# A vision tower on one core: the expert row buffer zeroed in another order, and unread products on TensorE behind the convolution

## The chip, the cores and the metric

The program runs on one of the eight cores of a Trainium2 chip, in one launch. The time is device microseconds of an execution, and a kernel's time is the median of its runs. Three runs of the kernel before took 235.38, 237.4 and 239.8 us, median 237.4.

## The reference

128 images of 64x64x3 go through a small vision tower. Each image gives 16 tokens of 128 features, 2048 tokens in all, everything in float32.

```python
y = conv(concat(x, four shifts of x), 16x16 patches) + conv_b     # 2048 x 128
h = layernorm(y) * gamma + beta;  h = h @ dense_w + dense_b
n = layernorm(h)                                                  # retention with 8 heads
h = h + silu(n @ wg.T + bg) * (decayed (q k') v)
n = layernorm(h)                                                  # 64 experts, top 2
buf[expert, position] = n   for both chosen experts (at most 256 rows each)
y = (silu(buf @ w1) * (buf @ w3)) @ w2                            # for each expert
h = h + weighted sum of the token's two expert rows + shared expert(n)
```

Rows of `buf` that no token fills are zero in the reference.

## The kernel before, in words

The program is written engine by engine, in an order set by hand; semaphores connect the engines. Nothing is scheduled by a planner.

**Attention phase.** The tokens form 16 tiles of 128. A loop of 21 steps (`for i in range(LAST)`) is written out on TensorE (PE), ScalarE (ACT), VectorE (DVE) and GpSimd (POOL). In step i, TensorE works on several tiles at different depths: `attend(i - 3)`, `embed(i + 1)` (lines 429 and 430), `places(i - 5)`, `scores(i - 2)` (line 473), `turn(i)` (two transposes, lines 441 and 444), `logits(i - 4)` (line 507) and `project(i - 1)` (lines 451 to 460). The convolution (line 419) is cut in four groups of four tiles, each of eight matmuls of 512 columns; `conv_step` puts two of them in each step, one at the step's start and one behind `turn`, so that group 1 is done in steps 0 to 2, group 2 in steps 3 to 6 and group 3 in steps 7 to 10. From step 11 on `conv_step` does nothing. A float32 matmul is two instructions in the trace.

GpSimd does in step i `rstd(i)` (lines 1054 to 1058: the inverse deviations of three layer norms, for which the vector engine and the scalar engine of the step wait), and then two `send(i - 6, k)` (line 1069): indirect DMAs that scatter a tile's 128 normalized rows to their places in the row buffer `buf` in DRAM (`expert_rows` in the trace), one for each of the two chosen experts. It works in order, so that a send that waits holds up the next `rstd`.

**The row buffer.** `buf` has 64 experts x 256 rows of 512 bytes (8 MiB), an overflow part and a drop part. It is zeroed from a tile of zeros, `fill` (128 partitions x 16 rows; the trace calls it EW, since it lies in that tensor), by DMAs that SyncE (SP) issues at line 328: eight, each on 128 partitions, where partition p writes rows 16n to 16n+15 of its own 128 rows. The first send waits for all eight (`pool.wait_ge(filled, 16 * FILLS)`). Before the fills SP waits for all four parts of the images of group 1 (`X` in three parts on 128 partitions, line 307, and `XE`, the edge pixels, on 96 partitions, line 309); the images of group 2 are issued behind the first fill, those of group 3 behind the last. SP's queue is worked off in order.

**Turnover.** Behind step 20 TensorE counts the rows of each expert (line 567). SP waits for all sends and then loads the rows of the first experts (line 352); the first transposes of the **expert phase** (line 575) wait for them. That phase takes 17 blocks of 4 experts through line 575 (transpose), 583 and 596, then comes the shared expert (lines 517 to 523), while GpSimd gathers the result rows (line 1097) and the output is stored.

Of the kernel before, what the change touches and what calls it, by code (L numbers as in the profile page):

```python
# [30 lines left out]
P = 128  # L31
# [68 lines left out]
def tower(nc, xp, xe, wp, we, sq, w13, w2, vecs, rows, cst, out):  # L100
    ctx = ExitStack()
    with ctx:
# [3 lines left out]
        def sem(name):  # L106
            return ctx.enter_context(nc.semaphore(name))
# [115 lines left out]
        wp_in = [sem(f"wp_in{n}") for n in range(NL)]  # L223
        x_in = [[sem(f"x_in{n}_{part}") for part in range(NL + 1)] for n in range(2)]
        filled_tile, filled = sem("filled_tile"), sem("filled")
        spare_filled, drop_filled = sem("spare_filled"), sem("drop_filled")
        ones_set = sem("ones_set")
        w_ready, wd_in_ready, wd_ps, wd_ready, cvec_ready, bqm_ready, before_ready = (sem(n) for n in (
            "w_ready", "wd_in_ready", "wd_ps", "wd_ready", "cvec_ready", "bqm_ready", "before_ready"))
# [55 lines left out]
        def turns(i):  # L285

            return min(max(i - FIRST2 + 1, 0), LAST2 - FIRST2 + 1)
        FILLS = NE * CAP // P // FILLR
        SPARES = NOV * BLK // P // FILLR
        PACE = 6  # L290
        assert FILLS * FILLR * P == NE * CAP and SPARES * FILLR * P == NOV * BLK

        def first_blocks(g):

# [4 lines left out]
        def _(sp):  # L299
# [16 lines left out]
            sp.dma_start(R[:, :], rows.partition_broadcast(P)).then_inc(r_in, 16)  # L316
            load_group(1)
            sp.dma_start(decay, cst[:, NC_CONST - NC_DECAY:]).then_inc(decay_in, 16)
            for part in range(NL + 1):
                sp.wait_ge(x_in[1][part], 16)  # L320
            sp.wait_ge(filled_tile, 1)
            sp.dma_start(buf[SLOTS:ROWS], fill[:, 0]).then_inc(drop_filled, 16)
            main = buf[0:NE * CAP].rearrange("(p r) w -> p r w", p=P)
            spare = buf[NE * CAP:SLOTS].rearrange("(p r) w -> p r w", p=P)
            for n in range(FILLS):
                if n == 1:
                    load_group(2)
                sp.dma_start(main[:, n * FILLR:(n + 1) * FILLR], fill[:, :, :]).then_inc(filled, 16)
            load_group(3)
            for n in range(SPARES):  # L330
                sp.wait_ge(y_ps, PACE + n)
# [2 lines left out]
            def load_weights():  # L334

                for n in range(NWL):
                    c = slice(n * WEX, (n + 1) * WEX)
                    sp.wait_ge(y_ps, PACE + SPARES + n)
                    sp.dma_start(EW[:, 0, c], w13[c].rearrange("e d n -> d e n")).then_inc(w13_in[n], 16)
                sp.wait_ge(w_ready, NL)  # L340
                sp.wait_ge(filled, 16 * FILLS)
                sp.wait_ge(spare_filled, 16 * SPARES)
                for n in range(NWL):
                    c = slice(n * WEX // PE_EX, (n + 1) * WEX // PE_EX)
                    sp.wait_ge(y_ps, PACE + SPARES + NWL + n)
                    sp.dma_start(EW[:, 1, c], w2.rearrange("(q a) h n -> (a h) q n", a=PE_EX)[:, c]
                                 ).then_inc(w2_in[n], 16)
# [56 lines left out]
        def _(pe):  # L404
            def conv(g, j):

                if j % HC == 0:
                    pe.wait_ge(x_in[g % 2][j // HC], 16 * (g // 2 + 1))
                    if g == 0 and j < NCH:
                        pe.wait_ge(w_ready, j // HC + 1)  # L410
                    if g == 0 and j == NCH:
                        pe.wait_ge(we_in, 16)
                if j == 0 and g >= 1:
                    pe.wait_ge(yT_ready, g)
                if j < NCH:
                    w, x = W[:, j], X[:, g % 2, j]
                else:
                    w, x = WE[:, j - NCH], XE[:, g % 2, j - NCH]
                mm = nc.tensor.matmul(CONV[:, :], w, x, start=(j == 0), stop=(j == NCH + 1))  # L419
                if j == NCH + 1:  # L420
                    mm.then_inc(conv_ps, 1)
# [112 lines left out]
            pe.wait_ge(wd_ready, 1)  # L534
            pe.wait_ge(cvec_ready, 1)

            def conv_step(i, n):

                g, j = (i + 1) // TG + 1, 2 * ((i + 1) % TG) + n
                if i == 0:  # L540
                    conv(g, n)
                if g < NG:
                    conv(g, j)

            embed(0)
            for i in range(LAST):
                conv_step(i, 0)
                if 0 <= i - 3 < NT:
                    attend(i - 3)
                if i + 1 < NT:  # L550
                    embed(i + 1)
                if 0 <= i - 5 < NT:
                    places(i - 5)
                if 0 <= i - 2 < NT:
                    scores(i - 2)
                if FIRST2 <= i <= LAST2:
                    turn(i)
                conv_step(i, 1)
                if 0 <= i - 4 < NT:
                    logits(i - 4)  # L560
                if 0 <= i - 1 < NT:
                    project(i - 1)
# [3 lines left out]
            for k in range(TOPK):  # L566
                mm = nc.tensor.matmul(O[:, 0:NE], ones[:, :], acc[:, NT % 3, k], start=(k == 0), stop=(k == TOPK - 1))
            mm.then_inc(count_ps, 1)

            def turn_rows(q, u, v=0, first=False, back=2):  # L570

# [447 lines left out]
        @block.gpsimd  # L1019
        def _(pool):  # L1020
            steps = [0]

            def own(ins):

                steps[0] += 1
                ins.then_inc(pool_step, 1)
                pool.wait_ge(pool_step, steps[0])

            pool.memset(fill[:, :, :], 0.0).then_inc(filled_tile, 1)
            pool.memset(mhalf[:, :], -0.5)  # L1030
            pool.memset(MV[:, :, :, :], 1.0)
            pool.memset(EPS[:, 0:1], LN_TOK)
            pool.memset(EPS[:, 1:3], LN)
            pool.memset(bvg[:, :], 0.0)
            own(pool.memset(ones[:, :], 1.0))
            pool.sem_inc(ones_set, 1)
            pool.wait_ge(c_in, 16)
            pool.memset(acc[:, 0, 1], 0.0)
            pool.tensor_scalar(acc[:, 0, 0], expert, CAP / P, None, ALU.mult).then_inc(base_ready, 1)

            def rstd(i):

                if i < NT:
                    pool.wait_ge(ystat, i + 1)
                if 0 <= i - 1 < NT:
                    pool.wait_ge(hstat, i)
                if 0 <= i - 4 < NT:
                    pool.wait_ge(h2stat, i - 3)
                if 0 <= i - 3 < NT:
                    pool.wait_ge(xn_ready, i - 2)  # L1050
                if 0 <= i - 6 < NT:
                    pool.wait_ge(xf_ready, i - 5)
                b = i % 2
                own(pool.tensor_tensor(VE[:, :], MV[:, b, :, 1], EPS[:, :], ALU.add))  # L1054
                own(pool.tensor_tensor(RS[:, b], VE[:, :], mhalf[:, :], ALU.pow))  # L1055
                pool.sem_inc(rs_ready, 1)
                for k in (1, 2):
                    ins = pool.tensor_scalar(NM[:, b, k:k + 1], MV[:, b, k, 0:1], RS[:, b, k:k + 1], -1.0,  # L1058
                                             ALU.mult, ALU.mult)
                ins.then_inc(nm_ready, 1)  # L1060

            def send(t, k):

                pool.wait_ge(slot_ready, t + 1)
                pool.wait_ge(xf_ready, t + 1)
                if t == 0:
                    pool.wait_ge(filled, 16 * FILLS)
                    pool.wait_ge(drop_filled, 16)
                pool.indirect_dma_start(  # L1069
                    buf, bass.IndirectOffsetOnAxis(ap=slots[:, k, t:t + 1], axis=0),  # L1070
                    xrow[:, t % XR], None).then_inc(sent[t % XR], 16)

            for i in range(LAST):
                if i <= LAST2:
                    rstd(i)
                if 0 <= i - 6 < NT:
                    for k in range(TOPK):
                        send(i - 6, k)
            for k in range(TOPK):
                send(NT - 1, k)  # L1080


            for q in range(OVER):
                pool.wait_ge(ys_ready, q + 1)
                pool.dma_start(first_blocks(group(q)), ys[:, q % NY]).then_inc(put[q % NY], 16)  # L1085
            more = pool.value_load(ovn[0:1, 0:1], min_val=0, max_val=NOV // EG - 1)
            for n in range(MORE):
                with pool.If(more > n):
                    pool.wait_ge(put_over, 16 * EG * (n + 2))
            pool.wait_ge(put_over, 16 * EG)  # L1090
            pool.wait_ge(put_late, 16 * (NB - 1 - OVER))
            for z in range(NY):
                pool.wait_ge(put[z], 16 * stores(NY * NB + z))
            pool.wait_ge(conv_ps, NG)
            for t in range(NT):
                for k in range(TOPK):
                    pool.indirect_dma_start(  # L1097
                        pr[:, t, k], None, buf,
                        bass.IndirectOffsetOnAxis(ap=slots[:, k, t:t + 1], axis=0)).then_inc(pr_in[t // TS], 16)
# [53 lines left out]
```

## Time and profile before

| | |
|---|---|
| runs | 235.38, 237.4, 239.8 us; median 237.4 |
| profiled execution | 236.28 us, its span 234.5 us |
| mean granted TensorE clock | 0.842 |
| TensorE matmul, busy | 163.5 us (70%) |
| VectorE, busy | 135.6 us (58%) |
| GpSimd, busy | 107.2 us (46%) |
| DMA | 42.96 MB, mean 183 GB/s |

The span runs from the first to the last instruction; 1.8 us of the execution's time lie around it. The page cuts the span into 40 slices of 5.86 us. The attention phase takes the slices up to about 136 us, the expert phase those from 143 to 182, and the gather the rest. The granted clock has two levels: 1.00 is 2.4 GHz and 0.50 is 1.2 GHz.

### The profile page before, as it was taken

What the parts mean: (1) busy time and instruction counts of PE and PEld (TensorE: products, weight loads), DVE (VectorE), ACT (ScalarE), POOL (GpSimd) and SP (SyncE); (2) the same over time, 40 slices, a digit from 0 to 9 for tenths busy, and PEclk for the clock granted to TensorE, in tenths of its full rate; (3) what the DMA queues carried; (4) which work ended last, traced back from release to release, by engine and by line L of the source; (5) the groups of instructions that cost most, each with busy time, mean ns of one, the idle gap of its engine ahead of it and who ended that gap; (6) DMA issues with size and microseconds to landing.
All of it is one profiled execution on the core that took longest, in us unless ns stands there. A gap on an engine that the chain in (4) does not pass through costs nothing.

```text
span 234.5 us, 4462 instructions
## 1 busy us (share of the span) xinstructions
PE 163.5 (70%) x1402; PEld 113.3 (48%) x1402; DVE 135.6 (58%) x487; ACT 83.7 (36%) x229; POOL 107.2 (46%) x169
## 2 busy tenths in 40 slices
PE   0888899997999987888988305999998655530000
PEld 0334455664666655656575204888887433320000
DVE  1525646684768898886447781577777422229222
ACT  2010565555256676653552202555554101100000
POOL 4004322225836666675446750133330077777760
PEclk9999999999599999975555555999999999995555
DMA  6999799999998744300000118699742612224421
GB/s 245 390 315 291 231 379 422 425 414 361 389 289 227 225 141 130 117 22 25 22 22 15 35 45 246 170 257 286 249 121 81 192 41 55 56 52 121 118 73 34
DMA packets 29213, 42.96 MB, mean 183 GB/s; under 512 B 2752, under 2 KB 21376, under 8 KB 27904
## 3 DMA queue, kind: packets, MB, share of 16 engines
q1 hardware_dynamic: 26176, 35.27, 45.0%
q0 software_dynamic: 3008, 7.34, 10.6%
q8 instruction: 13, 0.21, 0.4%
q14 instruction: 16, 0.13, 0.2%
HBM read 24.45 MB, written 18.15 MB: 182 GB/s over the span
## 4 chain that ended last, share of the span: by engine, by line
PE 32%; DMA 21%; POOL 14%; issue 10%; DVE 8%; SPq 8%; ACT 3%; POOLq 1%; DVEq 0%; ACTq 0%
POOL X L1097 12%; DMA expert_rows<-EW 10%; DMA XE<-xe 6%; PE bank L583 5%; PE scores L484 5%; PE bank L575 4%; PE scores L473 3%; PE conv_counts L419 3%; DVE go L837 2%; SPq L307 2%; DMA expert_rows<-ys 2%; PE bank L459 2%; PE bank L507 2%; POOL expert_rows L1069 2%; PE scores L596 2%
## 5 line engine op out<-in xcount | busy, mean ns | idle before, releaser
L1097 POOL DMA_INDIRECT X<-expert_rows,slots x32 | 30.6, 956 | 21.8 <-DMA expert_rows<-ys 12.3
L1069 POOL DMA_INDIRECT expert_rows<-xrow,slots x32 | 32.4, 1013 | 14.6 <-issue 8.3
L419 PE MATMUL conv_counts<-X,W 128*128 128x512 f32 x48 | 26.9, 666 | 8.0 <-DVE W L776 6.6
L688 ACT ACTIVATE qm<-bank,bqm,C 128x128 f32<-128x128 f32 x64 | 24.1, 460 | 7.0 <-PE bank L452 7.0
L484 PEld LDWEIGHTS scores<-vg,ST 64*64 64x64 f32 x512 | 19.4, 156 | 10.2 <-issue 10.2
L973 DVE TENSOR_TENSOR hT<-bank,gs 64x256 f32<-64x256 f32 x34 | 14.5, 427 | 15.1 <-ACT gs L745 14.7
L1085 POOL DMA_DIRECT2D expert_rows<-ys x12 | 9.1, 762 | 27.5 <-DVE ys L987 27.5
L484 PE MATMUL scores<-vg,ST 64*64 64x16 f32 x512 | 20.9, 222 | 0.7 <-DVE ST L884 0.2
L1054 POOL TENSOR_TENSOR VE<-MV,EPS 128x3 f32<-128x3 f32 x20 | 4.0, 199 | 36.6 <-issue 15.2
L1055 POOL TENSOR_TENSOR RS<-VE,mhalf 128x3 f32<-128x3 f32 x20 | 17.8, 889 | 1.6
L837 DVE TENSOR_TENSOR go<-scores,vg 64x128 f32<-64x128 f32 x32 | 9.1, 286 | 15.3 <-PE scores L484 15.1
L583 PE MATMUL bank<-xbT,EW 128*128 128x128 f32 x128 | 17.9, 285 | 0.0
L737 ACT ACTIVATE xbT<-bank 128x512 f32<-128x512 f32 x17 | 10.2, 597 | 20.5 <-PE bank L575 20.5
L575 PE MATMUL bank<-C,xb 128*128 128x128 f32 x68 | 11.7, 302 | 7.4 <-DMA xb<-expert_rows 7.4
L661 ACT ACTIVATE xT<-bank 128x256 f32<-128x256 f32 (+1 forms) x19 | 6.7, 351 | 28.0 <-PE bank L444 22.6
L583 PEld LDWEIGHTS bank<-xbT,EW 128*128 128x128 f32 x128 | 16.4, 200 | 0.4 <-issue 0.3
L1010 DVE SCALAR_TENSOR_TENSOR h<-X,pw,h 128x128 f32<-128x128 f32 x32 | 9.5, 349 | 11.7 <-DMA X<-expert_rows,slots 9.6
L419 PEld LDWEIGHTS conv_counts<-X,W 128*128 128x128 f32 x48 | 8.6, 212 | 15.1 <-DMA X<-xp 11.4
L473 PE MATMUL scores<-qm,kT 64*64 64x256 f32 x128 | 12.5, 462 | 4.6 <-DVE go L837 4.5
L745 ACT ACTIVATE gs<-bank 64x512 f32<-64x512 f32 x17 | 10.0, 589 | 6.7 <-PE bank L583 6.6
L575 PEld LDWEIGHTS bank<-C,xb 128*128 128x128 f32 x68 | 7.8, 150 | 9.4 <-DMA xb<-expert_rows 7.6
L1058 POOL TENSOR_SCALAR NM<-MV,RS 128x1 f32<-128x1 f32 x40 | 10.3, 271 | 4.2 <-POOL RS L1055 4.2
(129 smaller groups left out, 338.1 us busy)
## 6 DMA issues: line engine op xcount, KB each, us to landing
expert_rows<-EW SPq DMA_DIRECT2D x10, 1024.0 KB, 17.8
X<-xp SPq DMA_DIRECT2D x12, 512.0 KB, 10.8
xb<-expert_rows SPq DMA_DIRECT2D x16, 256.0 KB, 4.1
expert_rows<-ys POOLq DMA_DIRECT2D x12, 256.0 KB, 3.3
EW<-w SPq DMA_DIRECT2D x4, 512.0 KB, 4.3
EW<-wp SPq DMA_DIRECT2D x3, 640.0 KB, 6.4
XE<-xe SPq DMA_DIRECT2D x4, 384.0 KB, 13.0
expert_rows<-ys SPq DMA_DIRECT2D x4, 256.0 KB, 3.0
```

What stands on the lines that cost most here:

```text
L419: mm = nc.tensor.matmul(CONV[:, :], w, x, start=(j == 0), stop=(j == NCH + 1))
L473: mm = nc.tensor.matmul(S[toks, n, 0:QM * TB], kT[rows, t % 2, toks], qm[rows, t % 2, :, toks], start=True, stop=True)
L484: mm = nc.tensor.matmul(S[toks, c, AVC + hh * HD:AVC + (hh + 1) * HD], ST[toks, t % 2, hh], vg[toks, t % 4, hh * HD:(hh + 1) * HD], start= ...
L575: mm = nc.tensor.transpose(XT[u][:, e * BLK:(e + 1) * BLK], xb[:, v, e], ident)
L583: mm = nc.tensor.matmul(GU[u][:, e * BLK:(e + 1) * BLK], w[:, e], xbT[:, u, e], start=True, stop=True)
L688: nc.scalar.activation(qm[:, t % 2, m], QK[:, 0:P], ACT.Identity, bias=bqm[:, m:m + 1], scale=head[:, m:m + 1])
L837: ins = nc.vector.tensor_tensor(go[toks], S[toks, c, AVC:AVC + P], vg[toks, t % 4, P:2 * P], ALU.mult)
L973: ins = nc.vector.tensor_tensor(hT[a * HID:(a + 1) * HID, u], up[:, a], gate[:, a], ALU.mult)
L1055: own(pool.tensor_tensor(RS[:, b], VE[:, :], mhalf[:, :], ALU.pow))
L1058: ins = pool.tensor_scalar(NM[:, b, k:k + 1], MV[:, b, k, 0:1], RS[:, b, k:k + 1], -1.0, ALU.mult, ALU.mult)
L1069: pool.indirect_dma_start(buf, bass.IndirectOffsetOnAxis(ap=slots[:, k, t:t + 1], axis=0), xrow[:, t % XR], None).then_inc(sent[t % XR], 16)
L1097: pool.indirect_dma_start(pr[:, t, k], None, buf, bass.IndirectOffsetOnAxis(ap=slots[:, k, t:t + 1], axis=0)).then_inc(pr_in[t // TS], 16)
```

## The change

There are two edits, and a few lines that serve them.

1. **The fills.** The same 8 MiB are now zeroed by 16 DMAs of 64 partitions. Each writes 16 rows of every one of the 64 experts; fill n takes its zeros from partitions 0 to 63 where n is even and 64 to 127 where it is odd. The first eight cover rows 0 to 127 of each expert and count on `filled`, the other eight count on a new semaphore `filled_rest`. The first send (tile 0) waits for the first eight alone, the sends of tile 1 for the rest; the load of the second projection's weights waits for both. SP begins the fills when two of the four parts of group 1's images have landed, no longer all four. The images of group 2 are issued behind two of the new fills, which is as many bytes as before; those of group 3 still behind the last.
2. **The products.** `idle_product` multiplies a convolution weight with 256 columns of weights (float32) into the PSUM bank of the convolution, and nothing reads the result. From step 11 on it stands in both places of `conv_step`; from step 16 on there is a third behind `places`; and 12 follow behind the count of rows. In all there are 37. The first waits for the last convolution result to be read out.

```diff
+        filled_rest, spare_filled, drop_filled = sem("filled_rest"), sem("spare_filled"), sem("drop_filled")
...
-        FILLS = NE * CAP // P // FILLR
+        FILLS = CAP // FILLR
+        FIRST_FILLS = P // FILLR
...
+        TURNOVER = 12
...
-            for part in range(NL + 1):
+            for part in range(NL - 1):
                 sp.wait_ge(x_in[1][part], 16)
...
-            main = buf[0:NE * CAP].rearrange("(p r) w -> p r w", p=P)
+            main = buf[0:NE * CAP].rearrange("(e r) w -> e r w", e=NE)
             for n in range(FILLS):
-                if n == 1:
+                if n == 2:
                     load_group(2)
-                sp.dma_start(main[:, n * FILLR:(n + 1) * FILLR], fill[:, :, :]).then_inc(filled, 16)
+                half = slice(n % 2 * NE, (n % 2 + 1) * NE)
+                sp.dma_start(main[:, n * FILLR:(n + 1) * FILLR], fill[half]
+                             ).then_inc(filled if n < FIRST_FILLS else filled_rest, 16)
             load_group(3)
...
+            def idle_product(i, n):
+                if i == NT - TG - 1 and n == 0:
+                    pe.wait_ge(yT_ready, NG)
+                nc.tensor.matmul(CONV[:, 0:2 * P], W[:, 0], W[:, 1:3], start=True, stop=True)
+
             def conv_step(i, n):
                 g, j = (i + 1) // TG + 1, 2 * ((i + 1) % TG) + n
+                if g >= NG:
+                    return idle_product(i, n)
...
                 if 0 <= i - 5 < NT:
                     places(i - 5)
+                if i >= NT:
+                    idle_product(i, 2)
...
             mm.then_inc(count_ps, 1)
+            for n in range(TURNOVER):
+                idle_product(LAST, n)
...
                 if t == 0:
-                    pool.wait_ge(filled, 16 * FILLS)
+                    pool.wait_ge(filled, 16 * FIRST_FILLS)
                     pool.wait_ge(drop_filled, 16)
+                if t == 1:
+                    pool.wait_ge(filled_rest, 16 * (FILLS - FIRST_FILLS))
```

The first place is SyncE's queue in the attention phase, from the wait for group 1's images to the load of group 3 (line 307 or 309 is X, 309 or 311 is XE, 328 or 331 the fills). Before:

```order
L322 DMA expert_rows<-EW 128x128 [waits x_in1_3,x_in1_2,filled_tile,x_in1_1,x_in1_0]
L328 DMA expert_rows<-EW 128x2048
L307 DMA X<-xp 128x1024 [waits conv_ps]
L307 DMA X<-xp 128x1024 x2
L309 DMA XE<-xe 96x1024
L328 DMA expert_rows<-EW 128x2048 x7
L307 DMA X<-xp 128x1024 [waits conv_ps]
```

Now:

```order
L324 DMA expert_rows<-EW 128x128 [waits filled_tile,x_in1_1,x_in1_0]
L331 DMA expert_rows<-EW 64x2048 x2
L309 DMA X<-xp 128x1024 [waits conv_ps]
L309 DMA X<-xp 128x1024 x2
L311 DMA XE<-xe 96x1024
L331 DMA expert_rows<-EW 64x2048 x14
L309 DMA X<-xp 128x1024 [waits conv_ps]
```

The order of the queue is the same; the fills are twice as many at half the partitions, and the queue starts on two parts of group 1.

The second place is TensorE in the second half of step 16 and the start of step 17. Before:

```order
L473 MATMUL scores<-qm,kT 64x256 x3
L441 MATMUL bank<-C,xrow 128x128 [waits xf_ready,th_ready,xT_ready]
L444 MATMUL bank<-C,xn 128x128 [waits xn_ready]
L507 MATMUL bank<-SQ,xT 128x64 [waits xT_ready]
L451 MATMUL bank<-xT,SQ 128x128 [waits qk_ready,xT_ready]
L452 MATMUL bank<-xT,SQ 128x128
L459 MATMUL bank<-SQ,xT 128x256 [waits g_ready,vg_ready]
L460 MATMUL bank<-bvg,ones 128x256
L484 MATMUL scores<-vg,ST 64x16 [waits st_ready,vg_ready]
```

Now:

```order
L546 MATMUL conv_counts<-W 128x256
L478 MATMUL scores<-qm,kT 64x256 [waits av_read,st_ready,qk_ready]
L478 MATMUL scores<-qm,kT 64x256 x3
L446 MATMUL bank<-C,xrow 128x128 [waits xf_ready,th_ready,xT_ready]
L449 MATMUL bank<-C,xn 128x128 [waits xn_ready]
L546 MATMUL conv_counts<-W 128x256
L512 MATMUL bank<-SQ,xT 128x64 [waits xT_ready]
L456 MATMUL bank<-xT,SQ 128x128 [waits qk_ready,xT_ready]
L457 MATMUL bank<-xT,SQ 128x128
L464 MATMUL bank<-SQ,xT 128x256 [waits g_ready,vg_ready]
L465 MATMUL bank<-bvg,ones 128x256
L546 MATMUL conv_counts<-W 128x256
```

Three products (L546) have come into a step: ahead of the scores, between the transposes and the logits, and ahead of the next step's attention matmuls (L484, L489 in the changed kernel).

## Rows read from the trace of the kernel before

**Rows 1.** Page, 40 slices of the span: TensorE's granted clock in tenths.

```profile
PEclk9999999999599999975555555999999999995555
```

**Rows 2.** Timeline at the first send: start, us, engine, line, operation, idle before.

```profile
48.08 0.16 DVE L863 SCALAR_TENSOR_TENSOR slots<-over,pos 128x2 uint32<-128x2 f32 x1
...
54.61 1.23 POOL L1069 DMA_INDIRECT expert_rows<-xrow,slots  x1 [5.42 <-DVE slots L863]
...
58.88 0.45 PE L429 MATMUL bank<-C,yT 128*128 128x128 f32 x1 [1.82 <-DVE h L871]
```

**Rows 3.** Timeline of PE: embedding matmuls of four steps, tiles 7 to 10.

```profile
51.01 0.39 PE L430 MATMUL bank<-WD,yT 128*128 128x128 f32 x2
...
59.12 0.63 PE L430 MATMUL bank<-WD,yT 128*128 128x128 f32 x2
...
67.40 0.39 PE L430 MATMUL bank<-WD,yT 128*128 128x128 f32 x2
...
73.19 0.39 PE L430 MATMUL bank<-WD,yT 128*128 128x128 f32 x2
```

**Rows 4.** Chain that ended last: start, us, what.

```profile
30.91 22.66 DMA expert_rows<-EW
```

**Rows 5.** Page, DMA issues: out<-in, queue, count, KB each, us to landing.

```profile
expert_rows<-EW SPq DMA_DIRECT2D x10, 1024.0 KB, 17.8
X<-xp SPq DMA_DIRECT2D x12, 512.0 KB, 10.8
...
XE<-xe SPq DMA_DIRECT2D x4, 384.0 KB, 13.0
```

**Rows 6.** Windows: us, busy time of each engine, clock, DMA share, GB/s.

```profile
45.00:50.00 5.00, 4.82 (x42) 2.92 (x40) 4.40 (x20) 2.68 (x9) 1.56 (x4) 1.00 1.01 421
20.50:22.50 2.00, 2.00 (x8) 1.02 (x7) 1.65 (x7) 0.00 (x0) 0.72 (x4) 1.00 1.01 209
32.00:33.50 1.50, 1.50 (x27) 0.74 (x27) 0.00 (x0) 1.50 (x7) 0.00 (x0) 1.00 0.92 276
55.50:57.00 1.50, 1.50 (x34) 1.01 (x32) 0.00 (x0) 1.09 (x5) 1.20 (x2) 1.00 1.09 243
```

**Rows 7.** Timeline of PE's weight loads: convolution matmuls that waited for image data.

```profile
20.11 0.30 PEld L419 LDWEIGHTS conv_counts<-X,W 128*128 128x128 f32 x2 [1.00 <-DMA X<-xp]
...
54.89 0.30 PEld L419 LDWEIGHTS conv_counts<-X,W 128*128 128x128 f32 x2 [0.47 <-DMA X<-xp]
```

**Rows 8.** Timeline: scores matmuls, last statistics, last send, first expert transpose.

```profile
95.67 0.66 PE L473 MATMUL scores<-qm,kT 64*64 64x256 f32 x8 [0.39 <-DVE go L837]
...
101.00 0.66 PE L473 MATMUL scores<-qm,kT 64*64 64x256 f32 x8 [0.39 <-DVE go L837]
...
122.92 1.13 PE L473 MATMUL scores<-qm,kT 64*64 64x256 f32 x8 [0.46 <-DVE go L837]
...
129.03 0.18 DVE L849 BATCH_NORM_AGGREGATE MV<-stats 128x2 f32<-128x6 f32 x1
...
137.93 0.96 POOL L1069 DMA_INDIRECT expert_rows<-xrow,slots  x1 [0.30 <-issue]
...
143.22 1.97 PE L575 MATMUL bank<-C,xb 128*128 128x128 f32 x8 [7.40 <-DMA xb<-expert_rows]
```

**Rows 9.** Windows: three in which the granted clock changed, and a full-clock stretch.

```profile
58.00:58.50 0.50, 0.00 (x0) 0.00 (x0) 0.12 (x1) 0.00 (x0) 0.30 (x1) 0.61 1.15 451
102.50:103.00 0.50, 0.50 (x3) 0.50 (x3) 0.43 (x2) 0.00 (x0) 0.42 (x2) 0.50 0.00 0
146.50:147.00 0.50, 0.50 (x5) 0.50 (x4) 0.00 (x0) 0.00 (x0) 0.00 (x0) 0.64 1.06 280
95.00:100.00 5.00, 3.93 (x58) 2.76 (x56) 4.51 (x21) 3.13 (x11) 3.32 (x6) 1.00 0.45 136
```

**Rows 10.** Timeline of PE: a 256-column f32 product and the matmul behind it.

```profile
76.27 0.60 PE L459 MATMUL bank<-SQ,xT 128*128 128x256 f32 x2
76.70 0.27 PE L460 MATMUL bank<-bvg,ones 96*128 96x256 bf16 x1
```

More of the change, by code:

```diff
@@ L225, in tower @@
         filled_tile, filled = sem("filled_tile"), sem("filled")
-        spare_filled, drop_filled = sem("spare_filled"), sem("drop_filled")
+        filled_rest, spare_filled, drop_filled = sem("filled_rest"), sem("spare_filled"), sem("drop_filled")
         ones_set = sem("ones_set")
@@ L287, in turns @@
             return min(max(i - FIRST2 + 1, 0), LAST2 - FIRST2 + 1)
-        FILLS = NE * CAP // P // FILLR
+        FILLS = CAP // FILLR
+        FIRST_FILLS = P // FILLR
         SPARES = NOV * BLK // P // FILLR
         PACE = 6
-        assert FILLS * FILLR * P == NE * CAP and SPARES * FILLR * P == NOV * BLK
+        TURNOVER = 12
+        assert FILLS * FILLR == CAP and SPARES * FILLR * P == NOV * BLK
         def first_blocks(g):
@@ L340, in load_weights @@
                 sp.wait_ge(w_ready, NL)
-                sp.wait_ge(filled, 16 * FILLS)
+                sp.wait_ge(filled, 16 * FIRST_FILLS)
+                sp.wait_ge(filled_rest, 16 * (FILLS - FIRST_FILLS))
                 sp.wait_ge(spare_filled, 16 * SPARES)
@@ L535, in _ @@
             pe.wait_ge(cvec_ready, 1)
+            def idle_product(i, n):
+                if i == NT - TG - 1 and n == 0:
+                    pe.wait_ge(yT_ready, NG)
+                nc.tensor.matmul(CONV[:, 0:2 * P], W[:, 0], W[:, 1:3], start=True, stop=True)
             def conv_step(i, n):
                 g, j = (i + 1) // TG + 1, 2 * ((i + 1) % TG) + n
+                if g >= NG:
+                    return idle_product(i, n)
                 if i == 0:
                     conv(g, n)
-                if g < NG:
-                    conv(g, j)
+                conv(g, j)
             embed(0)
```

## The prediction

> **What bounds the kernel now.** I read the page's slices first: TensorE's granted clock stands at full speed except in one slice near 60 us, in the seven from about 103 to 146 us, and at the end [rows 1]. The timeline of the embedding matmuls then gives the length of a step: tiles 9 and 10 are 5.79 us apart, which is a step with two convolution matmuls on a full TensorE; but tiles 7 to 9 took 16.39 us instead of 11.58, so 4.8 us were lost between 51 and 67 us [rows 3]. The timeline around the first send says why: its slots were written by 48.24 us, but it started at 54.61, because the chain of waits has the last fill issued at 30.91 and landed at 53.57 [rows 2, 4]. Behind that send stands the next `rstd`; TensorE sat idle 1.82 us for what it gives, and between 58.0 and 58.5 the clock went from 2.4 to 1.2 GHz [rows 2, 9]. From step 11 on, at full clock, a step takes 5.33 us: scores at 95.67 and 101.00 [rows 8]. There VectorE, busy 4.51 of 5 us, sets the pace, and TensorE waits for it (0.39 us ahead of the scores) [rows 8, 9]. At 102.5 the clock halved with no long pause before it [rows 9], and TensorE became the bound: three steps took 21.92 us, 101.00 to 122.92 [rows 8]. The expert phase begins at 143.22, when the last sends have landed and the rows are loaded, at half clock until about 146.6 [rows 8, 9].
>
> **Fills, the wait that goes.** If group 3's images and the fills come in time, the 4.8 us are all gained: the sends themselves (2.6 us a step on GpSimd) also stand in the steps of 5.79.
>
> **Fills, the wait that may come.** All hangs on the rate of a DMA on 64 partitions, which the trace doesn't have. Two bounds: DMAs on 128 partitions move 421 GB/s, and the loads of XE, on 96, were each time a dip with the DMA engines as busy as ever: 209, 276 and 243 GB/s, mean 243 [rows 6]. The packets of X and XE have the same length, so what differs is the partitions. A 64-partition fill should alone be no better than the lowest, 209. But fills alternate between halves, and an engine that has run ahead finds the other half free, so some of the way to 421 may be regained. I take **250**, nearest to the XE rows, and keep 209 and 421 as ends.
>
> SP may start at about 20.1 us, when TensorE's wait for the second part of group 1 ended [rows 7]; but the DMA engines are busy with XE until 22.5 [rows 6] and then with 0.3 MB of decay constants and drop rows, so I count from 23.4. A fill is 64 x 16 x 512 bytes = 0.524 MB; a part of X the same; XE 0.39 MB [rows 5]. At 250 GB/s for fills and XE and 410 for X: two fills 4.2 us (27.6), X of group 2 3.8 (31.4), XE 1.6 (33.0), six fills 12.6 (45.6), eight fills 16.8 (62.4), the first part of group 3 1.3 (**63.7**). The first send, asked for at about 49.3, waits no more. The sends of tile 1, asked for at about 55, wait to 62.4, and what is queued behind them is `rstd(8)`; but the images are later still. TensorE wants group 3 at 54.4 (it stood 0.47 us for it and started at 54.89 [rows 7]), and would now stand until 63.7, **9.3 us**. Everything of the step is behind this matmul, since TensorE works in order. After a pause of this kind the clock is at half; before, the pause cost 2.3 us up to tile 8, and the slow stretch behind it another 2.5 [rows 3], which I charge again. Tile 9 then comes at 62.6 + 9.3 + 2.5 = 74.4 instead of 67.40: **+7.0 us**. At 421 for fills and 243 for XE the first part of group 3 lands at about 50.4, before it is wanted: **-4.8**. At 209 it lands at 70.4: tile 9 at 81.1, **+13.7**.
>
> The Trainium skill (SBUF — State Buffer, "Door 1: The DMA port swizzle") says that partitions 0 to 63 reach only 8 of SBUF's 16 ports, gives 196 GB/s for 64 partitions against 328 for 128 at 1 MiB with an asymptote of 218, and says that two DMAs on the two halves still serialize. It speaks against this change; the dips at XE agree with it, no row of before has a 64-partition DMA. By 218 the first part of group 3 would come at 68.8 and the time would be an estimated 241.3.
>
> **The products while the clock is full.** One costs 0.43 us of TensorE (a 256-column float32 matmul to the next) [rows 10]. The one behind `turn` lies beside ScalarE's copy of the transposes, for which TensorE idles about as long. The one ahead of the attention matmuls delays them 0.2 to 0.3 us, which VectorE's pace hides in steps 12 to 14. The first waits for the last read-out of the convolution: up to 0.5 us once, I charge **0.3**.
>
> **The products and the clock.** The clock fell at 102.5 with TensorE busy 79% of the stretch before it, and did not fall in the convolution steps, where it was busy 96% [rows 9, 6]. The products bring 0.86 us of work into a step of 5.33, where two convolution matmuls had brought 1.7. I take it that the clock holds through steps 11 to 20. Then steps 15 to 17 take no more than 5.33 us each, 16.0 instead of 21.92: **-5.9**. From the scores of tile 15 (122.92) to its last statistics (129.21) there are 6.3 us, with one set of attention matmuls at 1.9 us for 1.1: **-0.8**. From the statistics to the last send (137.93) GpSimd is the chain (an `rstd` and six sends), and from there to 143.22 two DMAs: no change. The 12 products last 5.2 us behind the count, which in the timeline began 7.7 us before the rows landed, so that a pause of 2.5 us is left, and in the pause of 1.82 us the clock went to half [rows 2, 9]; of the 1.7 us that 3.4 us at half clock can cost, I take **-0.7**, ends 0 and -1.7. What is late next is the expert rows themselves, which no product moves. Together **-7.1**.
>
> The expert phase behind it, the shared expert and the gather run as before.
>
> **Sum.** 236.28 (the profiled execution, 1.1 below the median) + 7.0 - 7.1 = **236 us**: both edits work as written, and the images of group 3, queued behind the fills, give back what the clock brings.
>
> **Rivals.**
> 1. **The halves run at full rate.** For it: fills follow each other without a gap, so that both halves can be in flight; the order of the queue is kept; every row of the 128-partition fills shows 410 to 421. Against it: the XE dips. Time 236.28 - 4.8 - 7.1 = **224.4**.
> 2. **Slower: the halves stay in step.** All engines are on the same half at any time, the rate is 209, and TensorE stands at group 3's first matmul until 70.4. Time 236.28 + 13.7 - 7.1 = **242.9**. Below about 250 GB/s the change is slower than before, above it faster; for it: the lowest dip, 2.0 us at 209 GB/s, is the bytes of one whole XE. The port rule cited above is this rival.
> 3. **The clock doesn't hold.** Products are paid at half clock (0.86 us each, one a step on the path, three steps) and the 7.1 don't come: 236.28 + 7.0 + 2.6 = **245.9**, or 234 with full-rate fills. Against it: TensorE nearly always busy at half clock got its clock back each time (146.6).
>
> **How the numbers follow.** Forecast (fills at 220 to 320 GB/s) 0.40, rival 1 0.38, rival 2 0.15, rival 3 0.07. A change of 2% is about what this measurement can tell: faster means below 232.7, slower above 242.1. Of the forecast's 0.40, 0.08 lies below 232.7 (fills at 280 or more, group 3 some 4 us earlier), 0.30 within, 0.02 above. Rival 1 is faster. Of rival 2, 0.11 is slower and 0.04 within; of rival 3, 0.05 slower and 0.02 within. So faster 0.46, same 0.36, slower 0.18. The range 223 to 242 leaves out 0.05 below and some 0.15 above; the forecast's own range is 231 to 240.
>
> **What would show it.** In the profile of the changed kernel: the DMA rate between 34 and 60 us (250 here; 410 and the matmul of group 3 without a wait for rival 1; 209 and a wait to 70 for rival 2); a long wait of TensorE for X at about 54 us; the first send without a wait for fills; a granted clock of 1.00 from step 11 to the count, and scores 5.3 us apart in steps 15 to 17; the first expert transpose 6.7 us sooner after the last embedding. I would be wrong by a term not listed if group 2's images came late (wanted at about 31.7, here 28.9), or if the products pushed the attention matmuls past VectorE's slack, which would show as steps over 5.33.

## The result, and the profile after

The changed kernel took 223.85 us (median of 4 runs, 222.81 to 225.16), the kernel before 236.59 beside it (4 runs, 235.38 to 239.8): ratio 0.948, 95% interval 0.940 to 0.956. The forecast was 236; what came was rival 1, 224.4. On another chip, where the kernel before takes 262.7 us, the same change gave only 0.986 (0.981 to 0.992); a section below is about that.

The page of the changed kernel: TensorE's granted clock in 40 slices, and SP's two kinds of fill and the images (KB each, us from issue to landing).

```profile
PEclk9999999999999999999999996999999999996555
...
expert_rows<-EW SPq DMA_DIRECT2D x16, 512.0 KB, 9.6
X<-xp SPq DMA_DIRECT2D x12, 512.0 KB, 10.6
```

The seven slices at half clock of [rows 1] are gone but for one. Now the question on which the forecast hung, the rate of DMAs on 64 partitions. Windows of the changed kernel, columns as in [rows 6]; the first is half fills, half other transfers, the other two are fills alone:

```profile
22.00:24.00 2.00, 2.00 (x6) 0.76 (x4) 1.83 (x7) 0.00 (x0) 1.20 (x2) 1.00 1.09 318
40.00:45.00 5.00, 4.70 (x47) 2.78 (x45) 3.64 (x15) 2.68 (x10) 1.64 (x4) 1.00 1.00 418
45.00:50.00 5.00, 4.82 (x48) 3.08 (x44) 4.08 (x19) 2.68 (x10) 1.56 (x4) 1.00 1.00 413
```

From 34 to 50 us the fills moved 414 GB/s, where the kernel before had 421 in its window of 45 to 50 us [rows 6]. GpSimd at the first send (start, us, engine, line, operation, idle before), and TensorE's first matmul of group 3:

```profile
49.05 0.50 POOL L1074 TENSOR_SCALAR NM<-MV,RS 128x1 f32<-128x1 f32 x2 [0.21 <-POOL RS L1071]
50.07 1.23 POOL L1087 DMA_INDIRECT expert_rows<-xrow,slots  x1 [0.52 <-issue]
```

```profile
55.87 1.12 PE L424 MATMUL conv_counts<-X,W 128*128 128x512 f32 x2 [0.70 <-DMA X<-xp]
```

The send waits for no fill (5.42 us in [rows 2]); TensorE waits 0.70 us for the images of group 3 where 9.3 were forecast. The embedding matmuls of tiles 7 to 10, to be held against [rows 3]:

```profile
51.38 0.39 PE L435 MATMUL bank<-WD,yT 128*128 128x128 f32 x2
58.13 0.39 PE L435 MATMUL bank<-WD,yT 128*128 128x128 f32 x2
63.92 0.39 PE L435 MATMUL bank<-WD,yT 128*128 128x128 f32 x2
69.71 0.39 PE L435 MATMUL bank<-WD,yT 128*128 128x128 f32 x2
```

Tile 9 comes at 63.92 for 67.40, 3.5 us sooner. Of the 4.8 lost before, 0.96 stayed in the step from 51.38 to 58.13 (6.75 for 5.79), where TensorE waits for group 3, and this run was 0.4 behind at tile 7. Now the late steps, the same places as [rows 8]: scores matmuls, last statistics, last send, first expert transpose.

```profile
97.66 0.66 PE L478 MATMUL scores<-qm,kT 64*64 64x256 f32 x8 [0.28 <-DVE go L853]
...
113.47 0.66 PE L478 MATMUL scores<-qm,kT 64*64 64x256 f32 x8
...
118.80 0.18 DVE L865 BATCH_NORM_AGGREGATE MV<-stats 128x2 f32<-128x6 f32 x1
...
127.95 0.96 POOL L1087 DMA_INDIRECT expert_rows<-xrow,slots  x1 [0.30 <-issue]
...
133.21 0.66 PE L591 MATMUL bank<-C,xb 128*128 128x128 f32 x4 [2.31 <-DMA xb<-expert_rows]
```

Three steps take 15.81 us for 21.92, the tail to the last statistics 5.33 for 6.11. The windows of the changed kernel that answer to [rows 9]:

```profile
95.00:100.00 5.00, 4.68 (x62) 3.40 (x61) 4.47 (x22) 3.27 (x11) 3.36 (x6) 1.00 0.21 68
133.50:134.00 0.50, 0.36 (x4) 0.13 (x2) 0.00 (x0) 0.10 (x1) 0.00 (x0) 0.98 0.94 249
134.00:137.00 3.00, 2.94 (x14) 2.94 (x15) 0.00 (x0) 1.18 (x3) 0.00 (x0) 0.50 1.00 280
```

With the products TensorE is busy 4.68 of 5 us for 3.93, and the clock is 1.00 through all steps. It falls once, at 134.0, after the wait of 2.31 us for the first expert's rows. The gather begins 11.0 us earlier, after a slightly shorter expert phase:

```profile
176.91 1.03 POOL L1115 DMA_INDIRECT X<-expert_rows,slots  x1 [11.55 <-DMA expert_rows<-ys]
```

The same line of the kernel before:

```profile
187.90 1.03 POOL L1097 DMA_INDIRECT X<-expert_rows,slots  x1 [12.35 <-DMA expert_rows<-ys]
```

From the first expert transpose to here it is 43.70 us for 44.68. All of it adds up: 3.5 (stall of the first send) + 6.1 (steps 15 to 17) + 0.8 (tail) + 1.0 (expert phase), less 0.4 (0.14 in the steps from tile 9 to the scores at 97.66, where the first product's wait lies, and 9.15 us from statistics to last send for 8.90) = 11.0, and the profiled executions are 11.1 apart (236.28 and 225.16). This sum is read from one pair of traces; the two edits were not run apart on a chip with these times.

The 1.0 us of the expert phase is not the clock's. The last down product (the third kind of matmul in a block) in the kernel before and in the changed one:

```profile
182.04 0.71 PE L596 MATMUL scores<-EW,hT 64*128 64x128 f32 x8 [1.02 <-DVE hT L973]
```

```profile
171.85 0.71 PE L612 MATMUL scores<-EW,hT 64*128 64x128 f32 x8 [1.02 <-DVE hT L989]
```

It comes 38.82 us behind the first expert transpose before and 38.64 now, so TensorE's blocks gained 0.2 us. The other 0.8 lies between it and the gather, where GpSimd waits 11.55 us for the last result rows to be stored, 12.35 before. The kernel with no products at the turnover (below) has 11.56 there too, so the 12 products are not its cause; what is, stays open.

### The profile page after: what moved, and what is told of

Read it like the earlier page. It is cut to its first block, busy times and chain, and to the rows that moved or that the text cites. A ratio compares the mean times of both kernels' runs of the same rounds, so it can differ in the third digit from the quotient of the medians.

```text
span 223.4 us, 4617 instructions
## 1 busy us (share of the span) xinstructions
PE 166.6 (75%) x1476; PEld 115.5 (52%) x1476; DVE 135.3 (61%) x487; ACT 83.7 (37%) x229; POOL 107.2 (48%) x169
## 4 chain that ended last, share of the span: by engine, by line
PE 35%; POOL 16%; DMA 15%; SPq 14%; issue 10%; DVE 4%; ACT 3%; POOLq 1%; DVEq 0%; ACTq 0%
POOL X L1115 13%; DMA X<-xp 11%; SPq L331 8%; PE bank L599 7%; PE bank L591 5%; PE scores L489 3%; PE conv_counts L424 3%; PE scores L478 3%; SPq L309 3%; PE scores L612 3%; DVE go L853 2%; PE conv_counts L546 2%; PE conv_counts L612 2%; POOL expert_rows L1087 2%; ACT qm L704 2%
## 5 line engine op out<-in xcount | busy, mean ns | idle before, releaser
L489 PEld LDWEIGHTS scores<-vg,ST 64*64 64x64 f32 x512 | 16.2, 134 | 9.4 <-issue 8.6
L546 PE MATMUL conv_counts<-W 128*128 128x256 f32 x74 | 20.7, 390 | 0.0
L489 PE MATMUL scores<-vg,ST 64*64 64x16 f32 x512 | 17.7, 207 | 0.6 <-DVE ST L900 0.6
L1026 DVE SCALAR_TENSOR_TENSOR h<-X,pw,h 128x128 f32<-128x128 f32 x32 | 9.5, 350 | 10.8 <-DMA X<-expert_rows,slots 8.6
L853 DVE TENSOR_TENSOR go<-scores,vg 64x128 f32<-64x128 f32 x32 | 9.2, 286 | 10.3 <-PE scores L489 10.0
L478 PE MATMUL scores<-qm,kT 64*64 64x256 f32 x128 | 10.6, 398 | 3.6 <-DVE go L853 3.4
L546 PEld LDWEIGHTS conv_counts<-W 128*128 128x128 f32 x74 | 12.2, 192 | 1.6 <-ACT yT L660 0.2
```

What stands on the lines that cost most here:

```text
L478: mm = nc.tensor.matmul(S[toks, n, 0:QM * TB], kT[rows, t % 2, toks], qm[rows, t % 2, :, toks], start=True, stop=True)
L489: mm = nc.tensor.matmul(S[toks, c, AVC + hh * HD:AVC + (hh + 1) * HD], ST[toks, t % 2, hh], vg[toks, t % 4, hh * HD:(hh + 1) * HD], start= ...
L546: nc.tensor.matmul(CONV[:, 0:2 * P], W[:, 0], W[:, 1:3], start=True, stop=True)
```

## The experiments

### The rate of the halves, and the parts one by one

These four ran on one chip, on which the kernel before took 262.65 us (19 runs, 259.88 to 264.81). Their expectations were worked out for a kernel before of 236.6 us, so that only differences and ratios can be held against them.

**All fills from partitions 0 to 63.** This leaves sizes, count and order of the DMAs as they are and takes away the alternation.

```diff
-                half = slice(n % 2 * NE, (n % 2 + 1) * NE)
+                half = slice(0, NE)
```

> All 16 fills take their zeros from partitions 0 to 63; everything else is the changed kernel. Theory (a fill on 64 partitions alone runs at half rate, and only the alternation of the halves brings the rate back to 410): between 34 us and the end of the fills the DMAs move about 210 GB/s, the 16 fills need some 40 us instead of 29, TensorE stands at the first matmul of group 3 until about 69 to 71 us, and the time is about 241 to 243 us. Rival (64 partitions are as fast as 128, and the dips at XE have another cause): 410 GB/s as in the changed kernel, no wait over 1 us for group 3, time 224 us.

Measured: 273.17 us (270.67 to 274.58), ratio 1.043 (1.026 to 1.061). Windows of this kernel, at the fills and at the stall behind them:

```profile
50.00:55.00 5.00, 3.18 (x50) 1.93 (x48) 2.57 (x11) 1.92 (x7) 2.19 (x2) 0.87 1.00 208
60.00:65.00 5.00, 0.00 (x0) 0.00 (x0) 0.00 (x0) 1.52 (x6) 0.00 (x0) 0.50 0.99 217
```

and its longest wait of TensorE (us in total, times, longest):

```profile
PE conv_counts L424 <- DMA X<-xp: 10.5, 1, 10.5
```

Fills on one half move 206 to 217 GB/s from 40 to 65 us; with the halves in turn, 408 to 426 (35 to 45 us) on this chip and the next as well. Fills on one half have half the rate, and with the halves in turn they have all of it. The stall of rival 2 is real and looks much as that rival described it: TensorE waits 10.5 us for group 3, until 70.24 us (rival 2 had 70.4), with the clock at half. It comes when all fills are on one half. The kernel is 10.5 us slower than the one before on this chip (273.17 for 262.65); the expectation had 4 to 6, and the whole change was not run on this chip.

**The fills alone** (the three kinds of `idle_product` taken out) **and the products alone** (the fills as before, 10 of 1024 KB):

> The new fills and waits, but no products. Theory (the two edits add up): the fills' part is the 3.5 us by which tile 9 came earlier in the trace of the changed kernel (67.40 before, 63.92 after), so about 233 us; the clock falls to half in one of the steps 13 to 16 as before. Rival (each edit works only with the other, since a steadier TensorE keeps the clock): 236 us or more.

> The fills and waits of before, with all 37 products. Theory (the edits add up): the stall at the first send stays (tile 9 near 67.4 us), the clock holds from step 11 to the count, time 236.6 - 7.6 = 229 us. Rival: most of the gain was the fills' and this stays at 233 or more.

Measured: fills alone 264.2 us, ratio 1.006 (1.000 to 1.011); products alone 257.8, ratio 0.987 (0.974 to 0.999). The fills were to gain some 3.5 us and gained nothing; the products were to gain 7.6 and gained 4.9. Neither edit gains here what it does in the first pair of traces.

**The changed kernel without the 12 products at the turnover** (`TURNOVER = 0` for 12):

> The changed kernel without the 12 products behind the count; the 25 in the steps stay. In the trace of the changed kernel the clock still fell at 134.0 us, 0.8 us into the first expert transposes, and was back at 137.2; the first block took 5.4 us from its first transpose to its first down product, 5.6 before. Theory: the 12 products gain next to nothing, 224 us. Rival (they shorten the slow stretch as the forecast had it, by 0.7 to 1.7 us): 224.6 to 225.6 us.

Measured: 260.59, ratio 0.995 (0.990 to 1.000). The whole change is not among these four, so this run does not give the worth of the 12 products; the next four have it, on another chip.

### The whole change where the kernel before takes 262.7 us

The experiments ran on three chips: the four above on one, the six of this section on a second, the last two on a third. Which chip gave the first result is not known. That the chip and not the hour makes the difference is therefore argued from the times: the second chip gave 262.66 us and, five minutes later, 262.76.

> The whole change once more, beside its parts on one chip. Halves theory (the fills leave in two halves side by side at about 414 GB/s, so the first send does not wait, and the products hold the clock at 1.00): where the kernel before takes 236.6 us, 223.9, ratio 0.948. Where the chip takes 262.6 us for the kernel before, as the chip of the first four experiments did, the two gains are the same in microseconds, 3.5 for the fills and 6 to 9 for the clock: ratio 0.955 to 0.965. Rival (the gain is that of one chip only, since the parts gave ratios of 1.006 and 0.987 on the other): the sum of the parts, ratio 0.99.

> The fills from the row buffer in two halves, no added product. Halves theory on a chip where the kernel before takes 236.6 us: the stall before the first send goes, tile 9 comes 3.5 us earlier, and the clock still falls in the steps behind, so 233 us, ratio 0.985; steps 10 to 16 then run partly at 0.50. Rival (the fills are the whole gain, since everything behind the first send moves with it): 226 us, ratio 0.955. If the chip is the slow one of the first experiments: ratio 1.00 to 1.01, as measured there.

> The added products alone, with the fills as in the kernel before. Halves theory on a chip where the kernel before takes 236.6 us: the stall of 4.8 us stays, the clock gain of 6.5 us comes, 230 us, ratio 0.973, granted clock 0.92 or more from 65 us on. Rival (the products help only where TensorE comes without a stall, the clock falls in the stall and the products keep it down): 236 us, ratio 1.00. If the chip is the slow one: ratio 0.985 as measured there.

The fourth kernel issued group 3 before the last four fills and had 18 products at the turnover:

```diff
+                if n == 12:
+                    load_group(3)
```

> The changed kernel with the loads of group 3 issued ahead of the last four fills, and 18 products at the turnover in place of 12. Halves theory: the wait of 0.7 to 1.1 us for group 3 goes, the last four fills land 2 to 3 us later but the first send at 50 us awaits only the first half of them; the 6 further products cover the wait for the first expert's rows, so the clock does not fall at 134 us and the first block runs at full rate: 1 to 3 us less than the whole change, 221 to 223 us on a chip that takes 236.6 for the kernel before. Rival (the first send now waits for its fills, since four of the eight that it awaits leave later): 1 to 3 us more than the whole change.

Another chip, but the kernel before again took 262.66 us. The whole change: 259.71, ratio 0.986 (0.981 to 0.992). Fills alone 264.42, 1.010 (1.002 to 1.017). Products alone 257.5, 0.979 (0.975 to 0.982). The combined one 261.44, 0.991 (0.987 to 0.996). So my expectation that the two gains are the same in microseconds there was wrong: the whole gains 3 us, not 10, and the fills in halves cost 1.8 us though they run at full rate. The fourth kernel's earlier load of group 3 does take the wait for its images away (no wait for X in that trace), its first send does not wait for fills either (49.39 us), its clock does not fall at the turnover, and it gains nothing; the two intervals overlap, so this run decides no more than that. By the medians the products alone are the fastest of the four on this chip.

What keeps the clock up can be read from the pages of this chip. The granted clock in 40 slices of some 6.5 us, of the kernel before, the fills alone, the products alone and the whole change:

```profile
PEclk9999999997999855555555556999999998555555
PEclk9999999999796555555555555999999998555555
PEclk9999999997998979598899579999999998555555
PEclk9999999959889597977989797999999995555555
```

The mean clocks are 0.777, 0.759, 0.861 and 0.843. So it is the products, and not the fills, that take away the long stretch at half clock; with the fills alone it starts even earlier (at about 82 us for 90). But the clock does not stay at 1.00 either: with the products it falls and comes back many times.

The traces show why the gain is small. Every step with sends in it is longer there. Here is a step of the whole change on that chip (its traced execution, 263.54 us, is the slowest of its four): the attend, both sends, and VectorE's product that reads the attend's output.

```profile
96.13 1.11 PE L489 MATMUL scores<-vg,ST 64*64 64x16 f32 x32
96.35 1.07 POOL L1087 DMA_INDIRECT expert_rows<-xrow,slots  x1 [0.26 <-issue]
97.72 0.96 POOL L1087 DMA_INDIRECT expert_rows<-xrow,slots  x1 [0.30 <-issue]
99.28 0.59 DVE L853 TENSOR_TENSOR go<-scores,vg 64x128 f32<-64x128 f32 x2 [1.80 <-remote]
```

And the same step of the changed kernel in the first result:

```profile
90.34 1.11 PE L489 MATMUL scores<-vg,ST 64*64 64x16 f32 x32
90.56 1.07 POOL L1087 DMA_INDIRECT expert_rows<-xrow,slots  x1 [0.26 <-issue]
91.61 0.57 DVE L853 TENSOR_TENSOR go<-scores,vg 64x128 f32<-64x128 f32 x2
91.93 0.96 POOL L1087 DMA_INDIRECT expert_rows<-xrow,slots  x1 [0.30 <-issue]
```

The attend ends at 91.45 here and the product begins at 91.61, before the second send. There the attend ends at 97.24 and the product begins at 99.28, 2.0 us later and 0.6 behind the end of the second send; "remote" says that the records name no releaser. Not all of VectorE stands still: three of its instructions for another tile ran from 96.60 to 97.48 us, beside the first send (not shown). Below, this late start is called the hold. Steps from product to product become 6.7 to 7.5 us, mostly 7.2 to 7.4, for 5.3; where the clock is at half as well, 8.5 to 9.0. Two more runs asked whether the sends do it, and how the kernel before fares.

> The kernel before, unchanged, for its trace on a chip where it takes 262.6 us: there the changed kernel's steps with two sends in them were 7.2 to 7.4 us apart (5.3 to 5.8 on the chip of the first result), since VectorE's product behind the attend began 1.3 to 1.9 us late, and the last send came at 149 us. Send theory (each step with sends has this hold, whatever the fills do): here too 7.2 to 7.4 us from the first step behind the first send on, none of it ahead of that send, and the last send at 149 to 152 us, so that the stall for the fills costs only about 1 us of the end. Rival (the hold comes from the queue of fills in two halves or from the products): steps of 5.8 us up to the fall of the clock, last send at 140 us.

```diff
-                    for k in range(TOPK):
+                    for k in range(1):
                         send(i - 6, k)
```

> The changed kernel with one of a token's two rows sent in place of both (the rows of the second choice are left out of the experts' input). Send theory: on a chip where the kernel before takes 262.6 us, the hold of VectorE behind the attend comes from the second send, so it goes, and the steps are 5.3 to 5.8 us apart, the last send at 126 to 132 us, the whole 235 to 243 us (the end with its gathers stays slow). Rival (the hold is there in every step whatever POOL issues): steps of 7.2 to 7.4 us as before, last send at 149 us, 258 us in all. On a chip where the kernel before takes 236.6 us both say 223 us, with steps of 5.3 us.

Measured: 262.76 us for the kernel before, and **242.89** with one send. A step of the kernel with one send:

```profile
97.24 1.11 PE L489 MATMUL scores<-vg,ST 64*64 64x16 f32 x32
97.46 1.07 POOL L1087 DMA_INDIRECT expert_rows<-xrow,slots  x1 [0.26 <-issue]
98.95 0.59 DVE L853 TENSOR_TENSOR go<-scores,vg 64x128 f32<-64x128 f32 x2 [0.37 <-PE scores L489]
```

The product begins 0.6 us behind the attend and 0.4 behind the send's end; steps are 5.8 us, the last send comes at 130.7 for 152.1 (whole change) and 150.5 (before). So the hold comes with the sends and most of it with the second, as the send theory had it. The 17 us between 259.71 and 242.89 are not the hold alone: the clock now stays at 1.00 from 46 to 106 us, and the tail, from the last product to the last send, is some 2 us shorter. In the kernel before on that chip, at half clock from 90 us on:

```profile
100.86 1.89 PE L484 MATMUL scores<-vg,ST 64*64 64x16 f32 x32
100.93 0.95 POOL L1069 DMA_INDIRECT expert_rows<-xrow,slots  x1 [0.30 <-issue]
102.80 0.59 DVE L837 TENSOR_TENSOR go<-scores,vg 64x128 f32<-64x128 f32 x2 [1.84 <-PE scores L484]
```

Its attend takes 1.89 us and so ends (102.75) behind the send (101.88), and the product follows at once. From 100 us on a step at half clock is 7.5 to 7.7 us long and has no hold; a step at full clock has the hold and takes 7.2. The clock, worth 2 us a step on the first chip (21.92 against 15.81 for three), is worth 0.3 to 0.5 there. The same goes for the stall. In the kernel before the first send comes at 54.25, behind the product of its step (51.55); with the fills in halves it comes at 49.81 and holds that product to 52.71, so the removed wait is replaced by one more step with a hold. And this hold does what the stall did: TensorE stands still 1.83 us ahead of the scores, and in the step behind it the clock is at half (0.50 from 54 to 60 us in the whole change; the kernel before has its own slow stretch behind the stall, at some 59 to 62).

```profile
53.45 1.13 PE L478 MATMUL scores<-qm,kT 64*64 64x256 f32 x8 [1.83 <-DVE go L853]
```

### A later second send

Two kernels let the second send of a step wait until VectorE's product has been made, in the changed kernel and in the kernel before.

```diff
                     for k in range(TOPK):
+                        if k == 1 and i - 3 < NT:
+                            pool.wait_ge(av_read, i - 2)
                         send(i - 6, k)
```

> The changed kernel, with POOL's second send of each step waiting until VectorE's product behind the attend (go) is done. Send theory (on these chips VectorE's product is held until the send that is in flight ends, about 0.5 us behind its end, and the second send catches it again): with a second send that starts behind the product only the hold by the first is left, so the steps are 5.8 us apart as with one send, the last send comes at 131 to 134 us, and the end with its gathers stays as slow as it is: 243 to 248 us where the kernel before takes 262.6, ratio 0.93 to 0.945. Rival (the hold belongs to the number of rows in flight, not to when they are issued): steps of 7.2 us again, 258 to 262 us, ratio 0.985 to 1.00. On the chip of the first result both say 224 us.

> The kernel before (its fills from partitions 0 to 127, no products) with the same later second send. Send theory with the two gains of the change as the first result showed them (3.5 us for the fills, 6.5 for the clock, eaten by the hold on these chips): the stall before the first send and the clock's fall in steps 10 to 16 are seen again, 8 to 12 us more than the changed kernel with the later send, 253 to 258 us, ratio 0.96 to 0.98. Rival (the change's gain is small on these chips for another reason, as more room in another stage): 2 to 4 us more than the changed kernel with the later send.

They ran on a third chip, where the kernel before took 232.91 us (13 runs, 226.99 to 236.6), so the remedy for the hold was not tried where the hold is. Measured: 225.53 us (4 runs, 224.90 to 226.56) with the change, ratio 0.971 (0.958 to 0.984) to the kernel before; 235.29 (11 runs, 230.76 to 240.93) without it. Both have the same sends. Their medians are 9.8 us apart, but single runs without the change lie 5 to 15 us above those with it, so the gain of the first result is seen again in kind and not in an exact size. Windows 95 to 110 us, the kernel without the change (its traced run took 239.55 us, one of the slower) and the one with it:

```profile
95.00:110.00 15.00, 14.05 (x118) 9.92 (x116) 9.50 (x41) 6.94 (x22) 7.24 (x12) 0.50 0.17 54
```

```profile
95.00:110.00 15.00, 13.90 (x176) 9.91 (x178) 12.71 (x56) 10.33 (x33) 10.01 (x18) 1.00 0.19 57
```

In the same 15 us TensorE runs 176 matmul instructions (14 of them products) for 118, at twice the clock. The spread of the kernel before goes with this clock too: its fastest run on this chip, 226.99 us, had a mean granted clock of 0.898, the one of 231.17 us 0.872, the one of 236.6 us 0.843. The four runs of the changed kernel with the later send, all at 0.92 to 0.94, lie within 1.7 us. So what the change is worth depends on how long the kernel before runs at half clock in the execution beside it: its fastest run on this chip is only 1.5 us behind the median of the changed kernel with the later send.

The products at the turnover can be read from all traces, by the time from the first expert transpose to the first gather: 43.7 and 42.5 us with 12 products on the two faster chips (44.7 and 45.1 without), 43.7 and 42.5 on the slower ones (45.1 to 46.0 without any product, 44.3 with those in the steps alone, 42.5 with 18). The 42.5 are the traces in which the clock did not fall at the turnover.

## What the prediction had right and wrong, point by point

- **The step that failed is "Fills, the wait that may come".** It took 250 GB/s for fills on 64 partitions and charged +7.0 us; they ran at 414, and the term was -3.5. That is 10.5 of the 10.8 us between the forecast and the profiled execution. The bound of 421 and the alternation were both in the text ("some of the way to 421 may be regained"); the wrong choice was to let the XE loads stand for them. A single load on 96 partitions did not tell how two neighbours on different halves run: with the halves in turn 414 GB/s, on one half 206 to 217. Why XE's loads dip to 209 to 276 GB/s [rows 6] no run here settles.
- The Trainium skill (SBUF — State Buffer, "Door 1: The DMA port swizzle" and, for the two halves together, "Can I just issue two DMAs to hit both halves?") was weighed as rival 2. Its figure for one half, an asymptote of 218 GB/s, agrees with the 206 to 217 measured with the fills all on one half. Its sentence that two DMAs on the two halves still serialize does not hold for this queue of fills: 414 GB/s from 34 to 50 us in the changed kernel, 385 to 434 in its single microseconds.
- **Fills, the wait that goes**: 4.8 said, 3.5 gained, since group 3's images still came 0.7 us late. Rival 1 had their first part landing at 50.4 (its own terms add up to 50.1); it was issued at 44.94 and landed at 55.83. Between 22 and 34 us the core moved 302 GB/s and from 50.0 to 55.8 it moved 324, less than the 410 to 421 of the sum, so that rival 1 was right in rate and sign and 5 us too early with the landing.
- **The products and the clock** held in mechanism and size for the steps: -5.9 forecast, -6.1 measured for steps 15 to 17; -0.8 and -0.8 for the tail. For the turnover they did not: -0.7 was forecast, and the clock fell all the same, for some 3 us (134.0 to 137.3; before, 143.2 to 146.7), so that the blocks gained 0.2; that the phase as a whole gained 1.0 is luck. The first product's wait was put at +0.3: the step in which it falls takes 5.48 us for 5.34 from scores to scores (76.18 to 81.66, before 79.66 to 85.00), so +0.14. No later step is longer than 5.34.
- **The range** of 223 to 242 took in the result, the forecast's own 231 to 240 did not: the chance of rival 1 (0.38) carried it, and "faster" was the likeliest outcome (0.46) by that chance and not by the forecast's mechanism. The range was well hedged; the number of 236 and the reason given for it were not right.
- What the prediction did not have is that the same program can run with VectorE's product held behind GpSimd's indirect sends. Where it does, both of its gains shrink, since the hold stands at the same place in the step as the slow attend and the stall did, and each hold is a pause of TensorE that can bring the clock down. That the second send makes it longer was shown by taking it away; what in the chip causes it was not.

## What to carry to other kernels

If a large transfer must be split over both halves of the partitions, let neighbours in the queue alternate: here that kept the rate (414 GB/s for 421), and all on one half cost half of it. A term that decides the sign deserves a row of its own kind: if the nearest row differs in two ways (96 partitions, and alone), give the other bound as much weight as the row. A gain that takes one wait out of a step is worth what the next wait in that step leaves of it, so look at who ends second, on more than one chip.

## What the hardware showed that was not expected

- Two DMAs on the two halves of the partitions, neighbours in one queue, ran at 414 GB/s together; on one half, 206 to 217.
- On two chips VectorE's product (L853) began 0.4 to 0.7 us behind the end of an indirect DMA's time on GpSimd, up to 2.0 us behind its operand, in steps at full clock, while other instructions of VectorE ran beside the first of the two DMAs; in the changed kernel where the first result was measured, and on the third chip with the later second send, it began within 0.2 us of its operand.
- The same two chips lose more at the end. The last of 32 gathers is issued at 239.8 us and the span ends at 261.7, 21.9 later (7.5 in the first result), since VectorE and ScalarE stand still for up to 9.65 and 15.7 us while the gathers are issued. One of these waits, whole change:

```profile
239.87 0.42 DVE L914 TENSOR_TENSOR h<-conv_counts,h 128x256 f32<-128x256 f32 x1 [9.65 <-remote]
```

  With one send a token this end was as long (220.7 to 241.0), so it is not left over from the sends. Its cause stays open.
